# A two-layer decoder on one core: six row normalizations move to ScalarE, the C columns and the router change their products, the sums stand two scans behind

## What is computed

```python
x = ln(x + mamba(x))                 # conv, silu, B/C/dt projections, selective scan with E=512, N=16
x = ln(x + softmax(ln_affine(sim)))  # sim from ctx_512 and x, 256 columns
x = ln(x + moe0(x))                  # 8 experts x 176, top 2 of a softmax router, shared 352
x = ln(x + hgrn(x))                  # silu/sigmoid gates, linear scan, rms norm, output product
x = ln(x + adjacency(ctx_512, x))    # top 76 of 256 per row
x = ln(x + moe1(x))                  # 8 experts x 128, top 2, shared 256, gated

# inside mamba, per batch
ssm_p = hs @ W_x                     # 512 -> 128 (dt) + 16 (Bm) + 16 (Cm)
state = exp(dts * A) * state + dts * Bm * hs
y     = sum over n of state[:, :, n] * Cm[n]
```

## Time and profile before

| | |
|---|---|
| median of 3 runs | 624.16 us |
| profiled execution, its own time | 622.0 us |
| span of its trace | 620.1 us |
| TensorE busy | 537.2 us (87%) |
| VectorE busy | 500.9 us (81%) |
| ScalarE busy | 431.4 us (70%) |
| GpSimd busy | 266.7 us (43%) |
| mean granted TensorE clock | 0.913 of full |
| chain that ended last | PE 55%, DVE 18%, ACT 8%, issue 6% |

### The profile page before, as it was taken

How to read it: one execution, slowest core, us unless ns; L and a number is a source line. 1 busy time by engine, 2 the same in 40 slices (tenths; PEclk the granted TensorE clock), 3 DMA queues, 4 the chain that set the end, 5 groups by cost and what they waited for, 6 DMA issues and landing times.

```text
span 620.1 us, 8967 instructions
## 1 busy us (share of the span) xinstructions
PE 537.2 (87%) x2504; PEld 386.8 (62%) x2504; DVE 500.9 (81%) x1133; ACT 431.4 (70%) x964; POOL 266.7 (43%) x418
## 2 busy tenths in 40 slices
PE   3976783899868899899999998899999999999766
PEld 2644562577645557767666676567676766776634
DVE  2099989999888796999998999999999996664332
ACT  2787678799858869988977777977768781451201
POOL 1097559247575344656423555525435521111010
PEclk9875595799869899889999999999999999999959
DMA  7393010472206440048217411650182056042000
GB/s 211 98 395 148 2 69 1 151 227 70 69 1 176 119 133 2 3 130 242 65 35 211 125 69 42 178 151 1 43 268 59 2 149 212 1 145 77 9 1 8
DMA packets 29968, 63.55 MB, mean 102 GB/s; under 512 B 4896, under 2 KB 8736, under 8 KB 29536
## 3 DMA queue, kind: packets, MB, share of 16 engines
q1 hardware_dynamic: 29920, 62.98, 33.2%
HBM read 61.85 MB, written 1.11 MB: 102 GB/s over the span
## 4 chain that ended last, share of the span: by engine, by line
PE 55%; DVE 18%; ACT 8%; issue 6%; POOL 1%; DVEq 0%; POOLq 0%; ACTq 0%
PE work L605 32%; PE work L655 12%; PE h_bank L581 5%; PE work L581 4%; DVE st L1154 4%; DVE acc L1170 3%; ACT dA L945 2%; DVE m L1119 2%; DVE wk L1123 2%; DVE h_tok L1072 1%; ACT L945 1%; ACT L816 1%; DVE bst L997 1%; DVE row L1004 1%; ACT xsT L816 1%
## 5 line engine op out<-in xcount | busy, mean ns | idle before, releaser
L543 POOL TENSOR_TENSOR dbu<-du,b_rows 128x512 f32<-128x512 f32 x128 | 163.0, 1274 | 87.6 <-DVE st L1154 67.8
L945 ACT ACTIVATE dA<-dts,a_neg 128x127 f32<-128x127 f32 x512 | 156.7, 355 | 13.0 <-DVE st L1154 11.8
L1154 DVE TENSOR_TENSOR_SCAN st<-dA,dbu 128x512 f32<-128x512 f32 x128 | 155.5, 1217 | 10.7 <-ACT dA L945 10.0
L581 PE MATMUL h_bank<-ident,st 128*128 128x128 f32 x512 | 91.3, 310 | 30.1 <-DVE st L1154 30.0
L605 PE MATMUL work<-stream,xsT 128*128 128x352 f32 x320 | 109.7, 485 | 4.7 <-DVE du L1088 1.8
L581 PEld LDWEIGHTS h_bank<-ident,st 128*128 128x128 f32 x512 | 68.7, 159 | 60.2 <-DVE st L1154 42.8
L1170 DVE SCALAR_TENSOR_TENSOR acc<-h_bank,c_cols,acc 128x512 f32<-128x512 f32 x128 | 93.5, 730 | 8.9 <-PE h_bank L581 6.8
L605 PEld LDWEIGHTS work<-stream,xsT 128*128 128x128 f32 x320 | 59.8, 199 | 35.3 <-issue 3.5
L488 POOL TENSOR_SCALAR var<-mv 128x1 f32<-128x1 f32 x56 | 12.7, 227 | 144.4 <-DVE mv L998 143.3
L816 ACT ACT_TABLE_LOAD x42 | 53.9, 1283 | 4.3 <-PE work L605 3.5
L655 PE MATMUL work<-stream,h_t 128*128 128x256 f32 x224 | 54.7, 390 | 0.8 <-ACT h_t L816 0.7
(11 more groups left out here) (159 smaller groups left out, 831.9 us busy)
## 6 DMA issues: line engine op xcount, KB each, us to landing
stream<-in_stream SPq DMA_DIRECT2D x80, 352.0 KB, 3.6
stream<-in_stream SPq DMA_DIRECT2D x32, 384.0 KB, 3.6
b_rows<-b_dram SPq DMA_DIRECT2D x32, 256.0 KB, 5.0
stream<-in_stream SPq DMA_DIRECT2D x8, 256.0 KB, 2.7
wg<-in_wg SPq DMA_DIRECT2D x1, 1280.0 KB, 9.3
wu<-in_wu SPq DMA_DIRECT2D x1, 1280.0 KB, 11.9
wd<-in_wd SPq DMA_DIRECT2D x1, 1280.0 KB, 14.6
xT<-in_xT SPq DMA_DIRECT2D x4, 256.0 KB, 4.5
```

The lines of the kernel that those rows point to most:

```text
L543: gp.tensor_tensor(tile, du[:, batch % 2, :, lo:hi], b_rows[:, b % 2, k:k + 1, :].to_broadcast([P, ET, P]), ALU.mult).then_inc(s["dbu_read ...
L581: return nc.tensor.transpose(dst, src, ident[:, :])
L945: last = A(dA[i % DA_RING][:, t, 1:P], dts[:, batch % 2, t, lo + 1:hi], ACT.Exp, scale=a_neg[:, t, k:k + 1])
L1154: V.tensor_tensor_scan(st[:, i % ST_RING].rearrange("p t l -> p (t l)"), dA[i % DA_RING].rearrange("p t l -> p (t l)"), dbu[:, i % DBU_RIN ...
```

## The change

- `normalize` moves from VectorE to ScalarE as one `Identity` activation with `scale=rstd` and `bias=shift`, where `shift` = -mean * rstd is one more GpSimd instruction behind the power (`root_of` with `mean`). VectorE gets waits for the row tile where it is about to write `r` again (`out` 4, `xat0` 2, the sums of both `ffn`, `hgrn` 5).
- The C columns: step `("pre", 3)` makes B and C together as 32 rows in `b_t`, and step `("pre", 4)` gets the columns with one transpose of 32x128 per half, behind a wait for the evacuation of `b_t`.
- The layer 0 router's 8 columns stand behind the 352 of the first gate chunk, so that its first product has 360 columns; tile `wr` and bank `logit0` are gone, and VectorE and ScalarE read the scores from the bank of `G0`.
- `LAG` = 2: in step k VectorE does the scan of state k and then the sum of state k - 2.
- `ORDER` and `BANK` are new.

```diff
@@ chains, ORDER
-        "s": [step for g in range(len(GROUPS)) for step in [("skip", g, 0)] + [("scan", g, k) for k in range(N + 1)]],
+        "s": [step for g in range(len(GROUPS)) for step in [("skip", g, 0)] + [("scan", g, k) for k in range(N + LAG)]],
...
     "dve": [
-        "saa0000111pppppppsssssssssssssssspssppppppssaas0s00ssssaassas0s0s0s00ss00a0pss00pppppps000aas000000ass0000000a",
+        "saa0000111pppppppssspsssssssssssssppppppsassaassss000sssssss0a0s000sssaasp00sppppppssas0s00000a000aaa000a00000",
...
@@ gpsimd, root_of
-                gp.tensor_tensor(rstd[layer][:, :], variance, mhalf[:, :], ALU.pow).then_inc(rstd_ready[layer], 1)
+                last = gp.tensor_tensor(rstd[layer][:, :], variance, mhalf[:, :], ALU.pow)
+                if mean is not None:
+                    links[0] += 1
+                    last.then_inc(s["pool_link"], 1)
+                    pool.wait_ge(s["pool_link"], links[0])
+                    last = gp.tensor_scalar(shift[layer][:, :], mean, rstd[layer][:, 0:1], -1.0, ALU.mult, ALU.mult)
+                last.then_inc(rstd_ready[layer], 1)
@@ tensor, ffn
+                elif k == 1 and lay == 0:
+                    pe.wait_ge(*read(xt, u))
+                    t = claim("G0_0", u)
+                    width = f.hi[0] + f.experts
+                    w = streamed("G0", u)
+                    fill(product(t, 0, lambda j: xsT[0][:, j, :], lambda j: w[:, j * width:(j + 1) * width], HT, width),
+                         "G0_0", u)
@@ tensor, pre 3 and 4
-                    fill(product(t[0:N], 0, lambda c: w_x[:, c, TR:TR + N], lambda c: hs[:, p, c, :], ET, L), "bT", b)
+                    fill(product(t[0:2 * N], 0, lambda c: w_x[:, c, TR:TR + 2 * N], lambda c: hs[:, p, c, :], ET, L), "bT", b)
...
+                    pe.wait_ge(*read("bT", b))
                     for lt in range(LT):
-                        last = product(t, lt * N, lambda c: hs[:, b % 2, c, lt * P:(lt + 1) * P],
-                                       lambda c: w_x[:, c, TR + N:TR + 2 * N], ET, N)
+                        last = nc.tensor.transpose(t[:, 2 * lt * N:2 * (lt + 1) * N],
+                                                   b_t[:, b % 2, lt * P:(lt + 1) * P], ident[0:2 * N, 0:2 * N])
@@ scalar
+            def normalize(key, i, u):
+                stage, k = key
+                layer = int(i > 3)
+                act.wait_ge(*root(stage, k, u))
+                A(rows(i, u), r[layer][:, :], ACT.Identity, scale=rstd[layer][:, 0:1], bias=shift[layer][:, 0:1])\
+                    .then_inc(row(i, u)[0], 1)
...
@@ vector, scan
-                    if k:
-                        n = k - 1
+                    if k >= LAG:
+                        n = k - LAG
```

More of the change, by code:

```diff
@@ L31 @@
 OFFERED = range(0, U - 2)
+LAG = 2
 GROUPS = [(b, lt, 1) for b in range(B) for lt in range(LT)]
@@ L91 @@
     "pe": [
[L92 to L95, removed]
@@ L281, in decoder @@
         ms = sb("ms", [P, 1])
+        shift = [sb(f"shift{i}", [P, 1]) for i in range(2)]
         rstd = [sb(f"rstd{i}", [P, 1]) for i in range(2)]
@@ L482, in _, with root_of @@
             links = [0]
-            def root_of(layer, variance, eps):
+            def root_of(layer, variance, eps, mean=None):
                 if eps:
@@ L740, in _ @@
                     turn_skip(b)
-                if stage == "scan":
-                    if k:
-                        turn_state(b, k - 1)
+                if stage == "scan" and 0 < k <= N:
+                    turn_state(b, k - 1)
                 if stage == "out" and k == 0:
@@ L819, in flat @@
                 return t.rearrange("p t l -> p (t l)")
+            def normalize(key, i, u):
[4 more added lines that the diff above has]
+                    .then_inc(row(i, u)[0], 1)
             def ffn(f, u, k):
                 lay = f.lay
+                if k == "norm":
+                    if lay == 0 and u >= 2:
+                        act.wait_ge(*row(4, u - 2))
+                    if lay == 1 and u:
+                        act.wait_ge(s["out_done"], 16 * u)
+                    normalize((f.stage, f.sum), (3, 6)[lay], u)
                 if k == 0:
@@ L998, in stats @@
                 V.bn_aggr(mv[layer][:, :], bst[layer][:, :]).then_inc(var_ready[layer], 1)
-            def normalize(key, i, u):
-                stage, k = key
-                layer = int(i > 3)
-                dve.wait_ge(*root(stage, k, u))
-                V.tensor_scalar(rows(i, u), r[layer][:, :], mv[layer][:, 0:1], rstd[layer][:, 0:1], ALU.subtract,
-                                ALU.mult).then_inc(row(i, u)[0], 1)
             def add_bank(n, u, rows_, layer=0):
@@ L1053, in ffn @@
                 elif k == f.sum:
+                    dve.wait_ge(*row(rows_in, u))
                     add_bank(f.stage, u, rows(rows_in, u), lay)
-                elif k == "norm":
-                    if lay == 0 and u >= 2:
-                        dve.wait_ge(*row(4, u - 2))
-                    if lay == 1 and u:
-                        dve.wait_ge(s["out_done"], 16 * u)
-                    normalize((f.stage, f.sum), rows_in + 1, u)
-                elif k != 0 and k[0] == "U":
+                elif k not in (0, "norm") and k[0] == "U":
                     c = int(k[1:])
```

127 lines of the change are left out of this document (73 added, 54 removed).

## The result

Before: median 623.88 us (622.72 to 624.46, 4 runs). The change: 630.47 us (629.48 to 635.94, 4 runs), ratio 1.0128 with a 95% interval of 1.0101 to 1.0155. The forecast was 612 us with a range of 599 to 624. The profiled execution took 630.32 us with a span of 628.5.

A forecast was written before the change was run, and what follows sets the result against it. VectorE led up to the 80th sum; from there to the last, TensorE was the nearer limit. 622.0 + 0.4 - 12.0 - 0.3 = 610.1 us; the median before lies 2.2 us above the profiled execution, so 612 us, range 599 to 624.

The forecast's parts named there:

- Point 1: Up to the 80th sum: moved work adds 5.9 us, the lag takes back 5.5 us of `h_bank` waits; net +0.4.
- Point 2: From the 80th to the last sum: VectorE has 21.7 us less work, which alone would give -21.7 us.
- Point 3: From the 80th to the last sum: TensorE, keeping 208.3 us, is the nearer limit; -12 us, ends -1.2 and -21.7.
- Point 4: C columns: 6 us in all, nearly all before the 80th sum, counted at nothing because VectorE's work covers it.
- Point 5: ScalarE: net +17.8 us, about 184 of 209 us between 80th and last sum; hidden behind TensorE and VectorE.
- Rival C: ScalarE becomes the queue: waiting rows delay exponentials and VectorE's scans; slower, 633 us as a median; chance 0.13.
- Point 7: Behind the last sum: longer row chain +1.4 us, TensorE's work there 1.7 us less; net -0.3 us.
- The rule that the forecast named: VectorE's `tensor_scalar` and GpSimd can contend for a port pair, held per instruction; ScalarE never waits; possibly 11.3 us of collisions.

The follow-up runs named there:

- row6_row3_late: As row6_late, with each unit's row 3 also moved behind the next unit's gate copy in ScalarE's order: 627.36 us, 1.0074.
- row6_late: The changed kernel with only each unit's last row normalization moved behind the next unit's x3T copy in ScalarE's order: 628.08 us, 1.0082.
- row6_late_scan_first: As row6_late, with 17 rows also moved behind the next scan exponential in ScalarE's order: 641.14 us, 1.0313.
- norms_on_vector: The changed kernel with its new orders, but the 48 row normalizations back on VectorE and no shift on GpSimd: 659.38 us, 1.0588.

## Why the prediction was wrong

- **Point 1, first stretch: the lag was right, the work mis-sized.** Forecast +0.4 us; the 80th sum came at 290.1 us, 3.7 us earlier, just inside the 290 to 297 that was named. VectorE's waits for `h_bank` are 0.7 us in the whole kernel, as forecast. But its busy time up to that sum rose by 0.9 us (243.5 to 244.3), and 5.9 were counted.
- **Point 2, VectorE's relief: its work was oversized by 6 us, and what was relieved wasn't used.** 15.8 us of VectorE's busy time left the second stretch (211.4 to 195.6), 21.7 were forecast. VectorE is busy 85% there, where 90 to 92% were forecast, and TensorE 92%, where over 97% were.
- **Point 3, "I take -12, leaving it about a microsecond": failed.** The stretch grew by 8.2 us. TensorE's busy time was 210.5 us where 208.3 were forecast, so the limit was nearly right; its idle time became 19.1 us where one was forecast. The step treated the engine with the most work as the one that sets the pace, and no term asked whose instructions it waits for. Its lower bound, -1.2, took it that the worst case is relief unused. It left out that a wait could be added. The router counted here as a gain of 1.8 us; in the old orders it cost about 12 over the whole kernel.
- **Point 4, C columns counted at nothing: nearly right in the mechanism, too small in the total.** Alone they are worth 3.9 us in the medians. In the profiled executions VectorE hid most of TensorE's saving, as the point said: of 7.4 us of TensorE's busy time 1.1 show at the 80th sum.
- **Point 5, ScalarE "Hidden behind TensorE and VectorE": this is the step that failed most.** The *busy* time was right (185.2 us in the second stretch, 184 forecast; 94 table loads; the row took 597 ns instead of 558). The point costed ScalarE's work and not its places in line. The waits in front of the rows, 43.9 us, appear in no busy share, and while they last the exponentials and the copies behind them are held. Not all of that waiting costs time (row6_row3_late has 9 us less of it than row6_late and is 0.7 us faster); what costs are the places where something ready stands behind the row, as at 495.83 us (2.9 us of TensorE) and at 588.27 (4.0 us of the final chain).
- **Rival C named this mechanism** and its price, 633 us, is 2.5 us off. The nearness of the number is luck: it took a loss of 0.6 us for each of 35 rows, which no run measured, and set against them a gain of 11.9 us that did not come. It got 0.13 because "ScalarE has 48 us of idle time in the second stretch, and the order can put a normalization late enough". Neither reason held: the idle time was there (44.4 us in that stretch, 229.7 less 185.2) and didn't help, and rows put later delay TensorE's transposes (row6_late_scan_first, +13 us over row6_late). The place was off too: C looked to the scans in the first stretches. Their waits are only 5.0 us longer in the whole kernel. More was lost at the copies x3T and `tf` and in front of TensorE.
- **Point 7, the end: -0.3 forecast, +3.9 measured.** Variance to row end is 1.9 us as forecast (1.8). What failed is that the tail was read as a chain of one unit. The last row of unit u and the first copy of unit u+1 were made by two engines before and are made by one now; moving that row behind the copy gives back 4.3 us.

So the step that failed is the "hidden" of point 5, and with it the -12 of point 3. In their place the runs show a row in line ahead of ready work. In the changed kernel that is worth 4.3 us of the tail in the profiled executions and 2.4 us in the medians. In the old orders the rows cost 17 us in all, and about 8.7 us is what the same wait at the head of the queue costs with instructions that nobody needs. How the changed kernel's 6.6 us divides between rows, router and orders is not settled: in its own orders, taking back the rows or the lag makes it slower still, and the router was not taken back there. The rows (17 us) and the router (about 12) cost more in the old orders than the whole change does in the new ones, so the new orders or the lag recover a good deal; which of the two does was not tried.

## What to carry to other kernels

An instruction that moves to an in-order engine brings its wait along: add up wait plus work at its new place and ask what stands ready behind it, not how busy the engine is. A small urgent product that is merged into a large one saves its own time, but its reader now waits for the large one, and the bank is held for both. And price each part alone, in the order that was fitted before: of the three edits tried so, rows, router and C columns, the plainest, the C columns, was the only gain (619.5 us, 0.6% faster than before), and beside the moved rows even that was gone.

## What the runs showed of the hardware

- ScalarE's `Identity` over 256 columns from SBUF with two pointer operands takes 584 to 611 ns, median 599; the instruction of this form that reads PSUM took 558. 144 columns took 497 to 501 ns in the mean. So 112 more columns cost about 97 ns, and by an estimate from these rows some 375 of the 500 ns don't depend on the columns.
- VectorE's normalization took 649 ns in the mean before and 434 ns in norms_on_vector, the same instruction and operands in another order; there 41 of the 48 waited for GpSimd's root first, and so began when GpSimd had just ended one:

```profile
L1031 DVE TENSOR_SCALAR row<-r,mv,rstd x48: 403/412/1212, 79.5 to 653.8; 128x256 f32<-128x256 f32 x48
```

  The median stayed (414 before) and the long ones became rare. The rule that the forecast named, from the page "SBUF — State Buffer" of the Trainium skill, section "Who interferes with whom", fits this, and fits that ScalarE's rows spread over 584 to 611 ns only. No run varied GpSimd's work by itself. When the rows left, VectorE's other instructions of this size did not get longer as a whole: four of its groups with two SBUF inputs of 256 columns (`r<-r,rstd,lnb`, `sisg<-tf,sisg`, `r<-r,ri,row`, `r<-row,g,S`) took 20.7 us before and 19.6 after.
